# Writing out the hardware loops of a graph-network kernel on every engine

## What is computed

```
edge_index = stack([src, dst])
h = maximum(layernorm(x), 0);  x = x + L0(h)   # own layernorm, Chebyshev convolution (K = 3), attention with 4 heads
h = maximum(layernorm(x), 0);  x = x + L1(h)   # messages mlp(x)[src] * mlp(edge_attr), summed by dst, layernorm
h = maximum(layernorm(x), 0);  x = x + L2(h)   # relu(x[src] @ W + b), summed by dst
h = maximum(layernorm(x), 0);  x = x + L3(h)   # [x_dst, x_src - x_dst] @ W.T, batch norm over edges, mean by dst
```

```
deg  = segment_sum(edge_weight, src)
dinv = where(deg > 0, 1 / sqrt(deg), 0)
w    = -(dinv[src] * edge_weight * dinv[dst])
prop(h) = segment_sum(w[:, None] * h[src], dst)
```

## Time and profile before

| | us |
|---|---|
| median of 3 runs | 8187.95 |
| fastest and slowest of them | 8158.64, 8191.77 |
| the profiled execution | 8203.84 |
| its span | 8201.9 |
| PE busy in it | 4544.7 (55%) |
| DVE busy | 4298.6 (52%) |
| POOL busy | 4255.4 (52%) |
| ACT busy | 2273.9 (28%) |

### The profile page before, as it was taken

How to read it: one execution, slowest core, us unless ns; L and a number is a source line. 1 busy time by engine, 2 the same in 40 slices (tenths; PEclk the granted TensorE clock), 3 DMA queues, 4 the chain that set the end, 5 groups by cost and what they waited for, 6 DMA issues and landing times. The chain is left out here.

```text
span 8201.9 us, 78150 instructions
## 1 busy us (share of the span) xinstructions
PE 4544.7 (55%) x17175; PEld 2185.1 (27%) x17176; DVE 4298.6 (52%) x6828; ACT 2273.9 (28%) x4663; POOL 4255.4 (52%) x3989
## 2 busy tenths in 40 slices
PE   2139946566565656657775553775885443555100
PEld 0014434344343433322221111332332111122000
DVE  1027745555554555534430008996996444787433
ACT  0000034444444422211112221232332112565211
POOL 6650044444444365556646652555664665665566
PEclk6569977777777767765556666887887555777555
DMA  0000022222222223321112222332232333222221
GB/s 12 0 0 17 0 72 86 86 90 88 85 86 85 90 66 73 78 51 50 50 50 70 76 75 67 101 103 58 77 82 72 104 102 91 58 64 55 60 63 51
DMA packets 444561, 541.92 MB, mean 66 GB/s; under 512 B 207490, under 2 KB 221960, under 8 KB 443641
## 3 DMA queue, kind: packets, MB, share of 16 engines
q1 hardware_dynamic: 319050, 449.36, 18.1%
q0 software_dynamic: 125440, 91.77, 5.7%
HBM read 302.04 MB, written 276.42 MB: 71 GB/s over the span
## 5 line engine op out<-in xcount | busy, mean ns | idle before, releaser
L1028 POOL DMA_INDIRECT l_got<-d_x,l_near x1176 | 1236.0, 1051 | 780.5 <-issue 384.2
L1028 POOL DMA_INDIRECT ln_xd<-in_x,ln_near x392 | 391.2, 998 | 1344.8 <-issue 865.5
L720 PE MATMUL ps<-hot_lo,hot_w 128*128 128x512 bf16 x2351 | 568.2, 406 | 441.2 <-issue 342.8
L1028 POOL DMA_INDIRECT p_got<-d_ext,p_near x392 | 399.5, 1019 | 348.1 <-DMA p_near<-in_src_rows 213.3
L662 DVE SCALAR_TENSOR_TENSOR hot_w<-iota_hi,hiS,vals 128x384 bf16<-128x384 bf16 x392 | 242.4, 618 | 589.2 <-remote 364.6
L1028 POOL DMA_INDIRECT p_got<-d_tx,p_near x392 | 399.4, 1019 | 275.1 <-issue 232.8
L1028 POOL DMA_INDIRECT p_got<-d_h,p_near x392 | 396.1, 1010 | 257.1 <-DMA p_near<-d_ls 134.2
L2218 POOL DMA_INDIRECT out<-fi_res,fi_near x392 | 381.6, 973 | 259.1 <-issue 171.7
L1187 DVE TENSOR_TENSOR_SCAN p_sums<-same,p_sums,ps 65x1024 f32<-65x1024 f32 (+3 forms) x98 | 229.4, 2341 | 498.7 <-remote 245.8
L606 POOL DMA_INDIRECT d_pos<-place,near x392 | 386.0, 985 | 167.8 <-issue 162.1
L1658 POOL TENSOR_TENSOR at_own<-at_hd,at_al 128x2048 f32<-128x2048 f32 x49 | 269.9, 5509 | 383.0 <-ACT at_al L1752 358.7
(11 more groups left out here) (371 smaller groups left out, 11827.7 us busy)
## 6 DMA issues: line engine op xcount, KB each, us to landing
d_x<-ln_x SPq DMA_DIRECT2D x196, 256.0 KB, 2.2
l_xd<-d_x SPq DMA_DIRECT2D x147, 256.0 KB
d_ext<-ln_ext SPq DMA_DIRECT2D x98, 264.0 KB
ln_x<-in_x SPq DMA_DIRECT2D x98, 256.0 KB
d_h<-ln_hb SPq DMA_DIRECT2D x98, 256.0 KB, 2.1
d_x<-l_x SPq DMA_DIRECT2D x98, 256.0 KB
out<-d_x SPq DMA_DIRECT2D x49, 512.0 KB
l_got<-d_x,l_near POOLq DMA_INDIRECT x1176
```

The source lines that it names most:

```text
L720: last = nc.tensor.matmul(bank(h), hot_w[:, r, k], hot_lo[:, r, 512 * h:512 * h + 512], start=False, stop=False)
L1028: nc.gpsimd.indirect_dma_start(out=out[:, q], out_offset=None, in_=source, in_offset=bass.IndirectOffsetOnAxis(ap=ids[:, q:q + 1], axis=0) ...
```

## The change

`ring_loop` gets a first branch that is always taken: all n + len(lags) - 1 steps are written out with `fixed`, and the loop behind it is never built. Group numbers, slots, row addresses and wait values are then Python integers, so that no register, no branch and no index arithmetic is left on any engine (POOL keeps a move for each indirect DMA), and a wait compares with a constant. `hold` raises HELD only where the value is not an integer, which no longer happens, so that no increment of HELD is left. The lines behind `ring_loop` move by 4, those behind `hold` by 6.

```diff
--- before.py
+++ after.py
@@ -94,6 +94,10 @@
             return (g // RING, g % RING, g) if 0 <= g < n else None
         step(at)
 
+    if UNROLLED[0]:
+        for s in range(n + len(lags) - 1):
+            fixed(s)
+        return
     for s in range(k_max):
         fixed(s)
     turns = (n - k_max) // RING
@@ -110,15 +114,17 @@
 def hold(eng, sem, value):
 
 
+    if not isinstance(value, int):
+        eng.wait_ge(sem, value)
+        eng.sem_inc(HELD[0], 1)
+    elif value > 0:
+        eng.wait_ge(sem, value)
+
+
+def after(eng, sem, value):
+
     if not (isinstance(value, int) and value < 1):
         eng.wait_ge(sem, value)
-        eng.sem_inc(HELD[0], 1)
-
-
-def after(eng, sem, value):
-
-    if not (isinstance(value, int) and value < 1):
-        eng.wait_ge(sem, value)
 
 
 def of_group(x, g):
@@ -130,7 +136,7 @@
     return i * 2 + r // 2
 
 
-HELD = [None]
+HELD, UNROLLED = [None], [True]
 
 
 class Norm:
```

## The result

The changed kernel took 8159.90 us (median of 18 runs, 8125.04 to 8189.75), the kernel before 8189.53 us (18 runs, 8156.62 to 8232.58): a ratio of 0.9966, 95% interval 0.9951 to 0.9981. That is a gain of 0.34%, within the 0.5% that the prediction called no change; it had forecast 7835 us and a range up to 8190. The direction was right and the size was not, by a factor of twelve.

What follows compares the result with a forecast made beforehand. POOL's indirect DMAs were the floor, with TensorE's late updates lifting phases off it. Savings of 132 + 33 + 39 + 61 + 16 + 37 + 35 = 353 us gave 7835 us against the median; range 7450 to 8190 us.

Steps and rivals of the forecast that it cites:

- What bounds the kernel: Whole kernel: POOL's gathers and scatters set the floor; waits for TensorE's late updates during POOL's indirect DMAs lift phases off it.
- the quarter: Late waits, all phases: one of four late updates goes, and a quarter of the wait; 258 of 353 us, lone_nodes 132.
- lateness stays whole: Rival: updates wait until POOL's burst drains, however many; only issue and POOL's relief gain, 85 us, 8103 us; chance 0.20.
- Degrees, POOL's relief: Degrees: scatters freed of POOL's slow sequencer instructions run at 1.28 us; 17 us gained after tiles missed.
- Lone nodes, issue: lone_nodes: half of PE's holds and the loop turns saved, 0.33 us for each of 98 groups, 33 us.
- Lone nodes, the wait at L341: lone_nodes: ACT's remote wait falls from 528.3 to about 400 us; next late is again the first L351 sum.
- Propagations: Both propagations: a quarter of the remote waits goes, 61 us in the first and 16 us in the second.
- The 4277 to 7604.8 us stretch: Attention, gated, relu and edge messages: 27 us from late updates at l_hf plus 10 us for issue.
- Finish: finish_rows: the 5.49 us gap per loop turn, put down to POOL's register waits, shrinks; 35 of 61 us.
- The cover I named: finish_rows: TensorE's late updates cost nothing, since they lie beside the scatters, which set the pace.
- The slower rival: Rival: the longer program is fetched in mid-phase, some 320 packets, costing up to 688 us, 8523 us; chance 0.09.
- Its other rule: Loops: a taken branch outside two instruction pages stalls for a fetch; forecast said the trace disagrees, adding nothing.

Runs made afterwards that it cites:

- paced_scatters_2: Changed kernel, but in degrees each group's scatters also wait until DVE has made that group's first tile; late updates: 7874.71 us, 0.9581 of before.
- no_dd: Changed kernel without the eight ln_dd gathers per pair (ln_dd set to 1); prompt updates 6210.15 us, 0.9929 of before; run again (_2), late: 7722.46 us, 0.9396.
- held_four: Changed kernel, everything written out, but each hold raises HELD four times; late updates: 8554.94 us, 1.0408 of before.
- bound_phases: Kernel before with only attention_sums, gated_messages and edge_convolution written out, on all engines; late updates: 8202.21 us, 1.0005 of before.
- unrolled_held: Changed kernel, all loops written out, but HELD still raised after each wait; prompt updates: 6247.13 us, 0.9991 of before; run again 0.9981.

## Why the prediction was wrong

- **What bounds the kernel.** Right in its place: TensorE's updates reach the others late while POOL issues indirect DMAs, and paced_scatters_2 and no_dd_2 took 355 and 504 us out by acting on POOL's stream alone. Not seen, and not to be seen in one profile: that this is a condition in which the same kernel takes 8190 instead of 6254 us.
- **The step that failed is the quarter**: "One of four late updates goes", and with it a quarter of the wait. It carried 258 of the 353 us. It took lateness for something that each update pays in its turn. The runs show a lateness that is common to all updates pending: in degrees the beat beside dense scatters is 16 to 17.5 us with two updates a tile (before), with one (after) and with five (held_four), and in lone_nodes the pending updates landed close together behind the burst, four of them within 0.18 us. So taking away updates bought nothing: lone_nodes took 37 us more where 132 less were forecast for this step, and degrees had 40 tiles at 560 us where 69 were expected. The beat was already in the trace of before; I had read only the average of 10.8 us a tile. The first rival, "lateness stays whole", had the mechanism, with 85 us forecast against 30 measured. I gave it 0.20 because tiles in degrees pass beside an unbroken stream. They do, but at a pace of POOL's making.
- **Degrees, POOL's relief.** Right as a cause (558.0 to 533.7 us), wrong in sign. I had charged the tiles missed in the shorter time, not that a denser stream lets through fewer updates in all the rest: 12 tiles fewer at 560 us, at 1.3 us each, are 16 us. With that cost the phase came out 9 us longer, not 17 shorter.
- **Lone nodes, issue**, 33 us. Not visible where updates are late. Where they are prompt 7 us of it show, 1070.8 to 1063.7 us, with the engines' own chain (1044 us in no_dd) and POOL's floor (1019) close below.
- **Lone nodes, the wait at L341.** It fell by more than forecast (230 us as the profile books it, 196 by idle time), and I had written that the next late thing would be the first L351 sum again. It was the second sum and the transposes of yb in the same burst, and the phase as a whole took 37 us more. That the written-out kernel is slower there than the loops holds in two profiles of each (1863 and 1879 against 1826 and 1817 us); why, no run isolates.
- **Propagations.** -60 us for a forecast of -77. Only the sum fits: p_sums lost 22 us of its remote wait, not 61, and the looped first propagation of bound_phases took 710.7 us, 16 less than in before with the same code. The 4277 to 7604.8 us stretch: -32 for -37; that may be luck too, with edge_convolution varying by 32 us.
- **Finish.** The slow instructions in POOL's sequencer were read rightly and went. The cover I named, "late updates lie beside the scatters", was false: POOL waits for fi_res at the same places, and its idle time before the scatters stayed at 259 us.
- **The slower rival** fell: 337 packets, close to the 320 estimated, and no stall for them. By the Trainium skill ("Runtime: NRT & Kernel Launch", "Instruction fetch mechanics") crossing into the next block is mostly hidden; the trace agrees. Its other rule is for a taken branch whose target is outside the window of two pages. The loops of lone_nodes showed no fetch at all, so they give it no case, and no sign that there was anything of that kind to gain: taking all branches away gave 0.34 and 0.36% together with the increments, and where updates are prompt unrolled_held, with no branch left, came to 0.9991 and 0.9981.

## What to carry to other kernels

Before pricing a wait that ends with a late update, ask what stream ends when the wait ends: in lone_nodes the long stalls closed just behind POOL's last gather, with the pending updates landing within 3 us, and in degrees the tiles kept one beat whatever was posted. That says which lever works, the stream's length and density, and not the number of updates. Look at single steps, too, before dividing by an average: 10.8 us a tile was a mix of steps from 17 down to 1.3. Relief of an engine that crowds others out can slow the kernel, so pace it by its consumers: one wait in degrees took 355 us out of that phase where updates are late, against 30 for the whole change. And time a baseline on more than one occasion before explaining a difference inside it.

## What the runs showed of the hardware

- The same kernel takes 6254 or 8190 us. In the late condition the updates of TensorE land some 14 us late behind a burst of 16 gathers (single ones up to 22) and 3 to 5 us late behind one of 8, while those of DVE and ACT that are on record land 0.01 us after the instruction's end. In the prompt condition TensorE's do so too, but for one at 1.3 us in the three phases looked at. What sets the condition, and whether the update or the matmul's completion is late, stays open.
- Updates that are pending at the end of a burst land close together: four of them within 0.18 us in the changed kernel's pair, three within 3.1 us in that of before.
- Beside dense scatters, TensorE's freed slots reach DVE one each 16.8 us, evenly (392.43, 409.22, 426.04 us), and one each 16 to 17.5 us with two or five updates a tile.
- In the late condition POOL's small sequencer instructions take some 0.7 us for stretches of degrees and finish_rows (moves of the degrees scatters: median 689 ns, in the prompt condition 29), but in lone_nodes 29 ns at the median. Without loops and increments they took 29 ns in degrees too, while TensorE's late updates remained. With the increments alone (held_four) the slow stretches were back: median 29, maximum 1422 ns.
- TensorE's clock goes with this: its mean granted clock was 0.70 in the late condition and 0.77 in the other. In degrees it was 0.99 throughout, the 2.4 GHz level, where TensorE had its tiles without gaps, and 0.57, near the 1.2 GHz level, beside the scatters when each tile waited for a late update.
- Some 270 instruction packets more (337 for 71), spread over 8 ms, showed no stall in the timelines, and the kernel with them was no slower.
